# Attention with two heads in the two row halves of TensorE, all value projections in the preamble, and DMA-packed results for the output projection

## The reference, cut to what matters

```python
q, k, v = (proj(Wq), proj(Wk), proj(Wv))          # B, 16 heads, T=1024, 16
att = einsum('bhqd,bhkd->bhqk', q, k) / sqrt(16)
att = where(causal, att, -inf)
att = softmax(att, axis=-1)
out = einsum('bhqk,bhkd->bhqd', att, v)
out = einsum('btc,dc->btd', out.reshape(B, T, 256), Wo)   # layer 1 adds a bias
```

## Time and profile before

| | |
|---|---|
| runs | 2340.90, 2348.93, 2356.53 us; median 2348.93 |
| profiled execution | 2359.97 us, of which the span is 2358.1 |
| busy: PE, DVE, ACT, POOL | 1968.2, 1624.1, 857.2, 455.3 us |
| mean granted TensorE clock | 0.901 of 2.4 GHz |

### The profile page before, as it was taken

The page is one execution under the profiler, slowest core; times in us unless marked ns, Lnnn a source line. Parts: engine busy times, 40 slices in busy tenths (PEclk is TensorE's granted clock), DMA queues, the critical chain, the costliest instruction groups (busy, mean ns, idle before and its releaser), DMA issues. The chain is left out here.

```text
span 2358.1 us, 28715 instructions
## 1 busy us (share of the span) xinstructions
PE 1968.2 (83%) x9912; PEld 1308.5 (55%) x9912; DVE 1624.1 (69%) x3486; ACT 857.2 (36%) x1599; POOL 455.3 (19%) x324
## 2 busy tenths in 40 slices
PE   6899998699999988856867385646789999999998
PEld 4455554488888856433433242323345555469998
DVE  3788881444444354789999989996477888156775
ACT  2265563222222222430122111110325556336775
POOL 0011110623033030001101100110001111015775
PEclk9699998899999999978988697777869999989999
DMA  4122220311010010100000000000112222028885
GB/s 159 35 58 58 58 57 11 125 36 56 34 53 18 0 54 30 59 1 9 10 10 0 18 9 9 0 0 3 48 41 49 57 59 57 11 66 252 231 235 123
DMA packets 62849, 129.63 MB, mean 55 GB/s; under 512 B 22792, under 2 KB 33800, under 8 KB 59904
## 3 DMA queue, kind: packets, MB, share of 16 engines
q1 hardware_dynamic: 53120, 115.04, 16.3%
q0 software_dynamic: 8832, 12.16, 3.0%
q10 hardware_dynamic: 768, 0.79, 0.1%
HBM read 91.27 MB, written 10.98 MB: 43 GB/s over the span
## 5 line engine op out<-in xcount | busy, mean ns | idle before, releaser
L713 DVE CUSTOM_DVE_ANT_0 pair<-pair,a_mask 128x512 f32<-128x512 f32 (+3 forms) x768 | 409.6, 581 | 113.3 <-PE pair L561 110.1
L677 ACT ACTIVATE a_prob<-pair 128x512 f32<-128x512 f32 (+3 forms) x768 | 329.7, 496 | 248.6 <-PE pair L585 244.4
L561 PE MATMUL pair<-a_kx,a_qx 96*128 96x512 f32 (+3 forms) x768 | 255.2, 400 | 33.3 <-DMA a_qx<-a_comp 19.8
L585 PE MATMUL pair<-a_qx,a_kx 98*128 98x512 f32 (+3 forms) x768 | 267.3, 395 | 6.6 <-ACT a_prob L677 5.7
L956 DVE TENSOR_TENSOR m_h<-pair,m_g 128x512 f32<-128x512 f32 x96 | 66.4, 691 | 215.3 <-PE pair L779 214.6
L585 PEld LDWEIGHTS pair<-a_qx,a_kx 98*128 98x128 f32 x768 | 143.9, 194 | 118.6 <-ACT a_prob L677 81.2
L516 POOL TENSOR_SCALAR_AFFINE_SELECT a_prob<-a_prob 128x512 f32<-128x512 f32 x128 | 82.3, 643 | 644.8 <-ACT a_prob L677 644.8
L1338 PE MATMUL pair<-h_stream,r_w_kz 128*128 128x512 f32 x192 | 106.9, 712 | 116.6 <-DVE r_region L1744 113.3
L561 PEld LDWEIGHTS pair<-a_kx,a_qx 96*128 96x128 f32 x768 | 152.5, 205 | 91.6 <-DVE a_mx_raw L713 47.8
L777 PE MATMUL pair<-m_x_hi,m_w_lo 128*128 128x512 f32 x448 | 177.5, 396 | 26.4 <-POOL m_w_lo L841 24.2
L779 PE MATMUL pair<-m_x_lo,m_w_hi 128*128 128x512 f32 x448 | 176.3, 393 | 0.0
(11 more groups left out here) (307 smaller groups left out, 4126.9 us busy)
## 6 DMA issues: line engine op xcount, KB each, us to landing
mx_raw<-in_L_ffn_experts SPq DMA_DIRECT2D x69, 512.0 KB
m_raw<-in_L_cond_experts SPq DMA_DIRECT2D x18, 1024.0 KB, 4.8
a_kx<-a_comp SPq DMA_DIRECT2D x96, 128.0 KB, 2.4
a_qx<-a_comp SPq DMA_DIRECT2D x360, 32.0 KB, 2.0
a_factor<-a_inverses SPq DMA_DIRECT2D x56, 128.0 KB, 2.7
r_w_ring<-in_r_q_w SPq DMA_DIRECT2D x8, 512.0 KB, 4.0
m_raw<-in_L_cond_experts SPq DMA_DIRECT2D x6, 512.0 KB, 3.7
token_rows<-mx_h_rows SPq DMA_DIRECT2D x2, 1040.0 KB, 8.6
```

The lines of the kernel that those rows point to most:

```text
L561: nc.tensor.matmul(first_bank[t % FR][:, 0:c1 - c0], qx[0:PRODUCT, m % 2, a, i * P:(i + 1) * P], kx[0:PRODUCT, m % 3, a // 2, c0:c1], star ...
L585: nc.tensor.matmul(score_bank[t % SR][:, q0:TT], kx[0:ROWS, n % 3, a // 2, j * P:(j + 1) * P], qx[0:ROWS, n % 2, a, h * TT + q0:(h + 1) * ...
L677: nc.scalar.activation(prob[:, i % RING, a, q0:TT], score_bank[t % SR][:, q0:TT], ACT.Exp, scale=SCALE).then_inc(s["b_exp"], 1)
L713: nc.vector.tensor_tensor_reduce(out=first_bank[t % FR][:, 0:cols], in0=first_bank[t % FR][:, 0:cols], in1=mask[:, m0:m0 + cols], scale=1. ...
```

## The change

Queries and keys of a head now fill 48 rows (the three products side by side), heads 0 and 2 at rows 0 to 47, heads 1 and 3 at rows 64 to 111, with the maxima's two rows behind them. So `first` and `scores` run on 48 and 50 rows in one half of the array's rows; `qx` has no zeros and needs half the planes. To fill them, four DMAs each do for keys and queries (`comp` has four planes: high, low, high, high; ScalarE writes planes 2 and 3 by one instruction of 2 x 512 and plane 0 by a second), and two for maxima. All four pairs' values are projected in the preamble, in four banks, and kept in `v_sb` with 17 columns for a head. `copy_values` and `copy_maxima` move from VectorE to ScalarE. The qk projections of groups 0 and 1 stand together ahead of the first pass, with banks of their own; group 1's parts lie in `prob`, which is free then. The normalised results of groups 0 to 5 are moved by four DMAs each into the half of a 128-row tile, two groups to a tile, so that an output projection has two terms (batch 0) or three (batch 1) for four; for the last quarter all but the last term are started in turn 7, in the banks of the first pass.

```diff
-PRODUCT = 3 * 2 * HD
+PRODUCT = 3 * HD
...
-SMALL = (("max", 0, 1), None, None, ("qk", 2, 0), ("qk", 2, 1), ("max", 1, 0), ("v", 0, 0), None, None, None, None, None)
-SMALL_LAST = (("max", 0, 1), None, ("out", 0, 0), None, ("out", 0, 1), ("out", 1, 0),
-              ("sums", 0, 0), ("spread", 0, 0), ("out", 1, 1), ("out", 2, 0), ("out", 2, 1), None)
+SMALL = (("max", 0, 1), None, None, ("qk", 2, 0), ("qk", 2, 1), ("max", 1, 0), None, None, None, None, None, None)
+SMALL_LAST = (("max", 0, 1), None, ("out", 0, 0), ("out", 0, 1), ("out", 1, 0), ("out", 1, 1),
+              ("sums", 0, 0), ("spread", 0, 0), None, ("out", 2, 0), ("out", 2, 1), ("begin", 3, 0))
+PACKED = NG - 2
...
 def before_turns():
...
     for h in range(HALF):
-        shared("qk", 0, h)
...
+        order += [("qk", 0, h), ("qk_use", 0, h), ("k_slots", 0, h), ("q_slots", 0, h)]
     for h in range(HALF):
...
+        order += [("qk", 1, h), *finished("qk", 1, h)]
+    order.append(("q_slots", 1, 1))
+    values = [(pair, v) for pair in range(NG // 2) for v in range(2)]
+    for f in range(NF):
+        order.append(("first", 0, f))
...
+        if f % 5 == 2 and values:
+            order += [("v", *values[0]), ("v_use", *values[0])]
+            values = values[1:]
...
+            if (i, a) == (4, 0) and 1 < n < PACKED + 2:
+                order.append(("pack", n - 2))
...
+        def rows_of(a, n):
+            return slice(a % 2 * 64, a % 2 * 64 + n)
...
+                    for a in range(GH):
+                        rows = slice(64 + a * HD, 64 + a * HD + HD)
+                        sp.dma_start(kx[rows_of(a, PRODUCT), m % 3, a // 2, t].bitcast(F32), parts(m)[rows, 0:3, t].bitcast(F32))\
+                            .then_inc(s["k_in" if m else f"k_first{h}"], 16)
...
+                def pack(n):
+                    sp.wait_ge(s["n_done"], n + 1)
+                    if n >= 2:
+                        sp.wait_ge(s["packed"], n // 2 * GH * 16)
+                    for a in range(GH):
+                        r0 = n % 2 * 64 + a * HD
+                        sp.dma_start(packed_pair(n // 2)[r0:r0 + HD, :], result_of(n)[a * SLOT:a * SLOT + HD, :]).then_inc(s["packed"], 16)
...
                 def v_projection(pair, v):
                     m = 2 * pair
-                    bank = take("v", pair, v)
+                    task = 2 * pair + v
+                    pe.wait_ge(s["used"], used("qk", 1, 1))
+                    if task >= len(v_banks):
+                        pe.wait_ge(s["v_used"], task - len(v_banks) + 1)
+                    bank = v_bank(pair, v)
...
-                    nc.tensor.matmul(first_bank[t % FR][:, 0:c1 - c0], qx[0:PRODUCT, m % 2, a, i * P:(i + 1) * P],
-                                     kx[0:PRODUCT, m % 3, a // 2, c0:c1], start=True, stop=True).then_inc(s["a_mm"], 1)
+                    r = rows_of(a, PRODUCT)
+                    nc.tensor.matmul(first_bank[t % FR][:, 0:c1 - c0], qx[r, m % 2, a // 2, i * P:(i + 1) * P],
+                                     kx[r, m % 3, a // 2, c0:c1], start=True, stop=True).then_inc(s["a_mm"], 1)
...
+                    r = rows_of(a, ROWS)
+                    nc.tensor.matmul(score_bank[t % SR][:, q0:TT], kx[r, n % 3, a // 2, j * P:(j + 1) * P],
+                                     qx[r, n % 2, a // 2, h * TT + q0:(h + 1) * TT], start=True, stop=True)\
                         .then_inc(s["b_mm"], 1)
...
+                def begin_out(t, _):
+                    pe.wait_ge(s["a_max"], NG * NF)
+                    pe.wait_ge(s["packed"], PACKED * GH * 16)
+                    pe.wait_ge(s["n_done"], NG - 1)
+                    for o in range(KD):
+                        for x, (weight, result) in enumerate(out_parts(t, o)[:-1]):
+                            nc.tensor.matmul(first_bank[o], weight, result, start=x == 0, stop=False)
...
+                    if t == NT - 1:
+                        nc.tensor.matmul(first_bank[o], *out_parts(t, o)[-1], start=False, stop=True).then_inc(s["om"], 1)
+                        return
...
-                    nc.scalar.activation(comp[:, 0, half(h)], bank_of("qk", m, h), ACT.Copy).then_inc(s["hi"], 1)
+                    to = parts(m)[:, :, half(h)]
+                    nc.scalar.activation(to[:, 2:4, :], bank_of("qk", m, h).unsqueeze(1).broadcast_to([P, 2, TT]), ACT.Copy)\
+                        .then_inc(s["hi"], 1)
+                    act.wait_ge(s["hi"], m * HALF + h + 1)
+                    nc.scalar.activation(to[:, 0, :], to[:, 2, :].bitcast(F32), ACT.Copy).then_inc(s["twin"], 1)
```

More of the change, by code:

```diff
@@ L266, in before_turns @@
     order = []
[L268 to L273, removed]
-    for h in range(HALF):
-        shared("qk", 0, h)
[L277 to L286, removed]
-    for h in range(HALF):
[L288 to L291, removed]
+    for h in range(HALF):
+        order += [("qk", 0, h), ("qk_use", 0, h), ("k_slots", 0, h), ("q_slots", 0, h)]
+    for h in range(HALF):
+        order += [("qk", 1, h), *finished("qk", 1, h)]
[3 more added lines that the diff above has]
+        order.append(("first", 0, f))
+        if f + 1 == MAX0:
+            order.append(("split", 0, 0))
+        if f + 1 == MAX0 + 3:
+            order.append(("max", 0, 0))
+        if f + 1 == MAX0 + 6:
+            order.append(("max_use", 0, 0))
+        if f % 5 == 2 and values:
+            order += [("v", *values[0]), ("v_use", *values[0])]
+            values = values[1:]
     order.append(("split", 0, 1))
@@ L299, in turn @@
     closing = m == NG
-    order, found, uses = ([] if closing else [("q_slots", m, 1)]), 0, []
+    order, found, uses = ([("q_slots", m, 1)] if 1 < m < NG else []), 0, []
     for i in range(NS):
@@ L381, in attention, with v_bank @@
     value_bank = banks[7]
+    early = {("qk", 0, 1): 0, ("qk", 1, 0): 1, ("qk", 1, 1): 2}
+    v_banks = [value_bank, *score_bank]
     def bank_of(*entry):
-        return shared_bank[BANK_OF[entry] % SB]
+        return score_bank[early[entry]] if entry in early else shared_bank[BANK_OF[entry] % SB]
+    def v_bank(pair, v):
+        return v_banks[(2 * pair + v) % len(v_banks)]
     def used(*entry):
@@ L496, in _ @@
                         norm(*which)
+                    elif what == "pack":
+                        pack(*which)
                     elif what == "split" and which == [NG - 1, 1]:
@@ L523, in take @@
                 def take(*entry):
-                    if used(*entry) > SB:
+                    if entry not in early and used(*entry) > SB:
                         pe.wait_ge(s["used"], used(*entry) - SB)
@@ L682, in copy_result @@
                     nc.scalar.activation(o_all[:, n * HALF + h, :], value_bank, ACT.Copy).then_inc(s["o_cp"], 1)
-                does = {"qk": upper, "q_slots": place_first_queries, "scores": probabilities, "copy": copy_result}
+                does = {"qk": upper, "q_slots": place_first_queries, "scores": probabilities, "copy": copy_result,
+                        "v_use": copy_values, "max_use": copy_maxima}
                 for what, *which in ORDER:
@@ L764, in add_result @@
                     tile = dest[:, o, half(t)]
-                    nc.vector.scalar_tensor_tensor(out=tile, in0=bank_of("out", t, o), scalar=bo[:, o:o + 1], in1=tile,
+                    bank = first_bank[o] if t == NT - 1 else bank_of("out", t, o)
+                    nc.vector.scalar_tensor_tensor(out=tile, in0=bank, scalar=bo[:, o:o + 1], in1=tile,
                                                    op0=ALU.add, op1=ALU.add).then_inc(s["used"], 1)
-                does = {"qk_use": lower, "v_use": copy_values, "first": maximum, "split": split_maxima, "max_use": copy_maxima,
+                does = {"qk_use": lower, "first": maximum, "split": split_maxima,
                         "sums_use": reciprocals, "spread_use": divide, "out_use": add_result, "norm": norm}
```

182 lines of the change are left out of this document (96 added, 86 removed).

## The result

The changed kernel takes 2380.28 us (median of four runs, 2375.76 to 2382.98) against 2352.66 us for the kernel before (four runs, 2340.90 to 2356.53): ratio 1.0132, 95% interval 1.0104 to 1.0160. The loss is small, but clear of the noise. The forecast was 2278, the range 2232 to 2318; both are missed on the far side. The profiled execution took 2375.76 us (span 2374.0, against 2358.1).

A forecast was written before the change was run, and what follows sets the result against it. TensorE's queue was taken to bound turns 0 to 6, VectorE second at 84%. Terms -12.5, -2.3, -1.6, -8.4, -4.2 and -6.5 gave -35.5 us an attention, -71 in all: 2278 us, range 2232 to 2318.

The forecast's parts named there:

- Row halves: Steady turns: half of neighbouring scores and firsts overlap in different row halves, 18.9 us for 22.7, -3.8 us a turn.
- ScalarE's place: Turns 0 to 5: double-width copy and twin ahead of the step's first exponential delay the fourth score, +2.6 us a turn.
- Changes of shape: Steady turns: four new changes of the array's shape (qk to scores, maxima to scores), 0.13 us each, +0.5 a turn.
- Values ahead: Turns 0 to 5: value projections moved to the preamble, -1.8 us a turn.
- rival D: Preamble gives the gain back: v at the low clock, turn 0 begins at 98 instead of 88; 2307 us; chance 0.07.
- Turn 6: Turn without v or `upper`: some of -3.3 us lost because VectorE is close to its bound, leaving -2.3 us.
- Turn 0: First turn: the 5.16 us wait for group 1's queries goes, with smaller gains, -8.4 us, 45.3 becomes 37.
- Turn 7: Last turn: 12 fewer output-projection instructions, -5.2, eight more shape changes, +1, together -4.2 us; scores win nothing.
- Tail: Last two projections after turn 7: two instructions each in banks of their own, -6.5 us.
- Rival A: Turns 0 to 6: row halves run side by side, ScalarE's delay is absorbed, VectorE becomes the bound; 2229 us; chance 0.20.
- Rival B: Turns 1 to 6: nothing gained from the row halves, turns stay as they are; 2307 us; chance 0.18.
- Rival C: Slower: weight loads wait for their own row half, up to 0.19 us per same-half neighbour; 2425 us; chance 0.07.

The follow-up runs named there:

- e5: Kernel before, with firsts and scores on rows 0 to 63 only, nothing else of the change; 2438.47 us, ratio 1.0343.
- e10: Kernel before, with firsts and scores on rows 0 to 31 only; 2491.57 us, ratio 1.0558.
- e2: Changed kernel, with firsts and scores over rows 0 to 111 (two heads' scores added), all waits kept; 2296.50 us, ratio 0.9755.
- e1: Changed kernel, with the second and third copies of the high part made by GpSimd instead of ScalarE; 2314.23 us, ratio 0.9851.
- e6: Changed kernel with both e2's rows 0 to 111 and e1's copies on GpSimd; 2269.23 us, ratio 0.9635.
- e3: Changed kernel, with six of the eight value projections back in turns 0 to 5; 2375.44 us, ratio 1.0094.
- e9: Kernel before, with only the firsts on rows 0 to 63, scores keeping 98 rows; 2544.92 us, ratio 1.0758.
- e12: Changed kernel, whole computation, with zero-filled 112 and 114 rows, GpSimd copies, six value projections in turns, packing in turns 6 and 7; 2279.72 us, ratio 0.9683.
- e11: e1 with only the firsts over rows 0 to 111, scores staying in row halves; 2398.68 us, ratio 1.0163.

## Why the prediction was wrong

**The step that failed** is the clock behind *Row halves*. The prediction priced the steady turns at the 1.00 that they had before, and in the preamble and turn 0 expected only the low clock of before. That a matmul on half the rows changes the granted clock was neither a term nor a rival. e5 shows it with nothing else changed, e10 strengthens it, and e2 takes it away with the change's order and waits kept.

How much of the miss it is, over the whole kernel: means of 0.901 and 0.868 make about 466 and 628 us at the lower level, and 162 us more there cost at most 81 (an estimate), against a miss of 102. In the first attention, turns 1 to 5: forecast 172.8 us (185.3 less 12.5), measured 197.6. At a full clock a turn of the changed kernel would take about 35.6 (an estimate: e1's 33.4 plus the 2.15 of ScalarE's place), five of them 178. So 5 us are mis-sized terms, and 20 are the clock. The preamble and turn 0 missed by another 25 us, and e2, with its rows, does not have most of that either: its first score starts at 83.46 (forecast 88, measured 95.98) and its turn 0 takes 39.0 us (forecast 37, measured 54.6). e2 is the changed kernel without the clock's fall, and without anything that the halves win; its 2296.5 lies 18 us above the forecast and inside the range.

Term by term:

- *Row halves, -3.8*: mis-sized. They start together, as said, yet at a full clock they bring 0.9 to 1.2 us a turn (e6 against e1, turns 1, 4 and 5), and in turn 6 about 1.4 (30.10 against e2's 31.45). That the loop of score, exponential and free bank holds the rest, which the prediction put 3.8 us lower, fits turn 7's steps, but was argued only.
- *ScalarE's place, +2.6*: right in kind, 2.15 measured. The rest of its price came through the clock: taking it away won 27 us with 112 rows (e2 to e6) and 66 with 50 (the changed kernel to e1).
- *Changes of shape, +0.5*: the price per change was right (0.13 taken, 0.15 measured). With four new ones a turn it stays small. The values' 1.00 us, which the prediction read as agreeing, says nothing of it: those eight instructions all have one shape.
- *Values ahead, -1.8*: right in kind in the turns, worthless as a whole, since the preamble pays. e3, with six fewer v in the preamble, starts turn 0 13.7 us sooner, 2.3 for each. That is nearer to the note's 2.7 at the lower clock than to the 0.9 that was taken: rival D's mechanism. The preamble (-1.6 forecast) came out at +6.4.
- *Turn 6, -2.3*: -2.4 measured, at a clock of 1.00. In the second attention, at 0.52, it was +12.4.
- *Turn 0, -8.4*: the DMA wait at its start went, as said. But it ran at 0.56 and took 54.6 us; in e6, at full rows and without the late exponential, the forecast's 37.0 came out (84.49 to 121.48).
- *Turn 7, -4.2*: -2.4, with the clock at 0.86 (0.94 before). In e2, at 1.00, it was -9.3: the fewer projections are worth more than I gave them. About 3 of the 9.3 are the clock, since 0.94 means 12% of 53 us at the lower level before (an estimate), which costs half of that.
- *Tail, -6.5*: -6.4 measured, at the lower clock. TensorE's last projections after, both of them, two instructions each:

```profile
433.54 3.75 PE L682 MATMUL pair<-a_o_all,w_qkv 128*128 128x512 f32 x4 [0.88 <-DVE a_o_all L804]
```

- Rival A falls: in e1's turns at full clock VectorE is busy for 28.4 of 33.2 us, and TensorE for 32.9. Rival B's price for the halves was the nearest one at a full clock. Rival C named the right sign and the wrong cause: loads on 64 rows don't wait. In e5's turn 1, at full clock, scores' weight loads (PEld) run beside the firsts' matmuls on the same rows:

```profile
147.58 0.82 PE L561 MATMUL pair<-a_kx,a_qx 64*128 64x384 f32 x2
...
148.02 0.41 PEld L585 LDWEIGHTS pair<-a_qx,a_kx 64*128 64x128 f32 x2
```

The first of the two loads is over (148.20) before the second first is (148.40). The Trainium skill ("TensorE: Matmul & The Clock Gate", Part 3) lets loads overlap only where the row group differs; e5, whose firsts and scores all use rows 0 to 63, shows again that they overlap here without that.

The signs that the prediction named for being wrong (turns at 31 or 37, loads behind the matmul, idle VectorE at each v) did not include turns of 36.9 and 41.6 in turn, which is what the clock makes.

## What to carry to other kernels

Where TensorE's granted clock stands at 1.00, list it as a term that the change can lose. Cutting a matmul's rows to about half saved nothing of its own time (e5's turn 1: 36.93 us for 36.28) and cost 3.4% of the kernel, most of it by the clock, so row halves want a count of what they win at a full clock first: here 0.9 us of 34.5. Keep neighbours in one shape, and put no late work ahead of the exponential that frees the next bank.

## What the runs showed of the hardware that I had not expected

- The granted clock goes with the rows that matmuls use (or with the array's shape, which changed with them): 1.00, 0.92 and about 0.80 of 2.4 GHz in turns 3 to 5 with 98, 64 and 32 rows, at the same instructions and columns. It falls with TensorE busy all the time (e10, e9). Rows filled with zeros serve to keep it up (e12: 1.00 in turns 1 to 7).
- Turns of the same work need not get the same clock: the changed kernel's turns 2 and 3 had 0.95 and 0.79, e9's 1.00 and 0.87.
- A change of the array's shape between neighbours costs 0.13 to 0.17 us (e9: 8.1 and 9.0 us for 54; e11: 7.5 us for 54 to 58).
- Waits of 0.8 and 0.4 us behind the two qk steps of a turn cost nothing of the clock with 112 rows (e2) and much with 50 (the changed kernel against e1). What sets the proportion was not separated further.
